# Late pointer columns of a graph-attention gather: one fp32 product per column becomes two bf16 products with row flags made four columns at a time

## What is computed

```python
hp = jnp.einsum('nf,hfo->hno', h, w)
e = leaky_relu(a_src[:, src] + a_dst[:, dst] + fc_b[0])
e = jnp.exp(e - seg_max.T[:, src])
att = e / seg_sum.T[:, src]
msg = att[:, :, None] * hp[:, dst, :]
agg = segment_sum(msg, src)        # for each head
```

## Time and profile before

| | us |
|---|---|
| median of 3 runs (12937.83 to 12961.71) | 12961.36 |
| profiled execution | 12922.84 |
| its span, first to last instruction | 12920.1 |

### The profile page before, as it was taken

The page is one execution under the profiler, slowest core; times in us unless marked ns, Lnnn a source line. Parts: engine busy times, 40 slices in busy tenths (PEclk is TensorE's granted clock), DMA queues, the critical chain, the costliest instruction groups (busy, mean ns, idle before and its releaser), DMA issues. The chain is left out here.

```text
span 12920.1 us, 83397 instructions
## 1 busy us (share of the span) xinstructions
PE 5468.6 (42%) x24919; PEld 3182.5 (25%) x25115; DVE 7098.3 (55%) x11439; ACT 3475.6 (27%) x4895; POOL 7317.1 (57%) x7495
## 2 busy tenths in 40 slices
PE   2224300029135555555537777777525665600001
PEld 1214300002124444444422222222112222200001
DVE  4663488889452222222227777777524655557761
ACT  0002333336013333333312222222100111156650
POOL 5645677758554444444455656556563455576654
PEclk5556655569556666666667777777757777755555
DMA  6101366635310000000011111111110111133431
GB/s 236 45 20 39 113 219 213 214 126 184 110 20 17 15 17 16 17 17 15 17 31 22 23 23 25 22 23 24 21 17 1 42 33 31 33 95 122 126 101 39
DMA packets 466533, 815.77 MB, mean 63 GB/s; under 512 B 229189, under 2 KB 326902, under 8 KB 415526
## 3 DMA queue, kind: packets, MB, share of 16 engines
q10 hardware_dynamic: 81600, 447.60, 8.9%
q0 software_dynamic: 236352, 156.57, 7.6%
q1 hardware_dynamic: 148134, 206.27, 4.9%
HBM read 402.58 MB, written 407.23 MB: 63 GB/s over the span
## 5 line engine op out<-in xcount | busy, mean ns | idle before, releaser
L1609 POOL DMA_INDIRECT hs<-tab_h,src_i x3136 | 2970.5, 947 | 2758.8 <-issue 1162.7
L1201 POOL DMA_INDIRECT en<-tab_s,src_i x1568 | 1569.8, 1001 | 857.3 <-issue 488.3
L1096 DVE SCALAR_TENSOR_TENSOR picked<-rank_ps,hot_hi 128x98 f32<-128x98 f32 x1568 | 313.2, 255 | 2113.8 <-remote 1123.5
L1888 PE MATMUL tp_ps<-w_pair,x 128*128 128x512 f32 x1568 | 1078.1, 776 | 534.5 <-DVE prod_b L2016 473.2
L2295 POOL DMA_INDIRECT rows_src<-out_rows,pos x784 | 750.6, 957 | 776.9 <-ACT out_rows L2338 503.1
L2317 PE MATMUL late_ps<-hot_col,hot_row 128*128 128x512 f32 x1120 | 760.6, 767 | 710.9 <-DVE hot_col L2396 626.1
L2307 POOL DMA_INDIRECT hs<-tab_h,ptr x784 | 741.3, 946 | 368.1 <-issue 252.1
L997 PE MATMUL rank_ps<-place_sb,hot_t 128*128 128x98 f32 x3136 | 843.3, 386 | 0.0
L2013 DVE TENSOR_TENSOR prod_a<-tp_ps,zz 128x768 f32<-128x768 f32 x392 | 374.6, 956 | 714.9 <-remote 563.2
L1035 PE MATMUL turn_bank<-place_sb,ident 128*128 128x98 f32 x784 | 231.7, 390 | 1196.0 <-issue 654.0
L997 PEld LDWEIGHTS rank_ps<-place_sb,hot_t 128*128 128x128 f32 x3136 | 685.5, 270 | 3.1
(11 more groups left out here) (396 smaller groups left out, 16043.0 us busy)
## 6 DMA issues: line engine op xcount, KB each, us to landing
sums<-rows ACTq DMA_DIRECT2D x98, 1088.0 KB
sums<-rows ACTq DMA_DIRECT2D x147, 512.0 KB
ev_rows<-zeros ACTq DMA_DIRECT2D x16, 3136.0 KB
en_rows<-en SPq DMA_DIRECT2D x49, 1024.0 KB
raw<-ev_rows ACTq DMA_DIRECT2D x49, 1024.0 KB
en_back<-en_rows ACTq DMA_DIRECT2D x49, 1024.0 KB
r<-in_edge_attr_2x ACTq DMA_DIRECT2D x49, 1024.0 KB
y_rows<-r ACTq DMA_DIRECT2D x49, 1024.0 KB
```

The lines of the kernel that those rows point to most:

```text
L1201: pool.indirect_dma_start(en[s][:, g, :], None, tab_s0, bass.IndirectOffsetOnAxis(ap=src_i[:, p * 2 * CH + g:p * 2 * CH + g + 1], axis=0)) ...
L1609: pool.indirect_dma_start(rows[k][:, g, :], None, tab_h, bass.IndirectOffsetOnAxis(ap=src_i[:, t * CH + g:t * CH + g + 1], axis=0)).then_i ...
L1888: nc.tensor.matmul(o, x2[k][:, a, b * EP:(b + 1) * EP], w3_cols, start=True, stop=False)
```

## The change

Each product of a late column becomes two bf16 products. The node number is split in two parts that are exact in bf16: `late_high`, a multiple of 128, and the rest, 0 to 127, which stays in `late_dst`. Four more small VectorE instructions on 560 columns make them once. Per four columns VectorE makes `row_flags` with one comparison (128x512 elements, bf16, ones and zeros). ScalarE multiplies the flags of a column by the high and by the low part (two instructions of 128 elements) into `hot_row`, which now has four buffers of two parts. `hot_col` is bf16, made as before, one instruction per column. TensorE runs four bf16 products per column (high and low, 512 and 272 columns). TensorE waits for two semaphores per column, ScalarE for the flags and for `late_added` to reach `n - 3`, VectorE ahead of new flags for ScalarE's rows of the four columns before. The number of late columns done ahead of the first turn and in each turn is rounded to a multiple of four: 148, and then 8 or 12 (mostly 8, 9 on average). ScalarE's share is placed ahead of its first turn and at the end of each turn.

```diff
-                hot_row = [sb(time, f"hot_row{n}", [EP, EP]) for n in range(2)]
-                hot_col = [sb(time, f"hot_col{n}", [EP, HCOLS]) for n in range(2)]
+                late_high = sb(time, "late_high", [EP, LATE])
+                row_flags = sb(time, "row_flags", [EP, LATE_GROUP, EP], BF16)
+                hot_row = [sb(time, f"hot_row{n}", [EP, 2, EP], BF16) for n in range(LATE_GROUP)]
+                hot_col = [sb(time, f"hot_col{n}", [EP, HCOLS], BF16) for n in range(2)]
...
-                return min(LATE, 150 + 9 * p)
+                return min(LATE, (150 + 9 * p) // LATE_GROUP * LATE_GROUP)
...
+                        pe.wait_ge(late_rows, n + 1)
                         pe.wait_ge(late_hot, n + 1)
-                        nc.tensor.matmul(late_ps[:, 0:512], hot_row[n % 2][:, :], hot_col[n % 2][:, 0:512], start=n == 0, stop=n == LATE - 1)
-                        nc.tensor.matmul(late_ps[:, 512:HCOLS], hot_row[n % 2][:, :], hot_col[n % 2][:, 512:HCOLS],
-                                         start=n == 0, stop=n == LATE - 1).then_inc(late_added, 1)
+                        for part in range(2):
+                            flags, begins, ends = hot_row[n % LATE_GROUP][:, part, :], n == 0 and part == 0, n == LATE - 1 and part == 1
+                            nc.tensor.matmul(late_ps[:, 0:512], flags, hot_col[n % 2][:, 0:512], start=begins, stop=ends)
+                            last = nc.tensor.matmul(late_ps[:, 512:HCOLS], flags, hot_col[n % 2][:, 512:HCOLS], start=begins, stop=ends)
+                        last.then_inc(late_added, 1)
...
                     H.lay(act, 2 * p + 1, 1, p)
+                    rows_of_late(late_by(p), late_by(p + 1))
+
+                def rows_of_late(first, end):
+
+                    for n in range(first, end):
+                        K.wait(act, "act", late_flagged, n // LATE_GROUP + 1, late_added, n - LATE_GROUP + 1)
+                        flags, made = row_flags[:, n % LATE_GROUP, :], hot_row[n % LATE_GROUP]
+                        nc.scalar.mul(made[:, 0, :], flags, late_high[:, n:n + 1])
+                        nc.scalar.mul(made[:, 1, :], flags, late_dst[:, n:n + 1]).then_inc(late_rows, 1)
+                rows_of_late(0, late_by(0))
...
+                        if n % LATE_GROUP == 0:
+                            K.wait(dve, "dve", late_rows, n)
+                            shape = [EP, LATE_GROUP, EP]
+                            nc.vector.tensor_tensor(row_flags[:, :, :], count_up[:, 0:EP].unsqueeze(1).to_broadcast(shape),
+                                                    pos_row[:, n:n + LATE_GROUP].unsqueeze(2).to_broadcast(shape), ALU.is_equal).then_inc(late_flagged, 1)
                         K.wait(dve, "dve", late_added, n - 1)
-                        nc.vector.tensor_scalar(hot_row[n % 2][:, :], count_up[:, 0:EP], pos_row[:, n:n + 1], late_dst[:, n:n + 1], ALU.is_equal, ALU.mult)
                         nc.vector.tensor_scalar(hot_col[n % 2][:, :], count_up, pos_late[:, n:n + 1], None, ALU.is_equal).then_inc(late_hot, 1)
```

More of the change, by code:

```diff
@@ L2201, in build @@
         with ExitStack() as st:
+            LATE_GROUP = 4
             own_e = [sb(st, f"own_e{n}", [EP, HEADS3, HCOLS]) for n in range(LISTS)]
@@ L2246, in build @@
             ptr_in, own_come, ptr_made = K.sem("ptr_in"), K.sem("own_come"), K.sem("ptr_made")
-            late_hot, late_added = K.sem("late_hot"), K.sem("late_added")
+            late_flagged, late_rows, late_hot, late_added = (K.sem(n) for n in ("late_flagged", "late_rows", "late_hot", "late_added"))
             rows_in = [K.sem(f"rows_in{s}") for s in range(2)]
```

4 lines of the change are left out of this document (added).

## The result

The changed kernel takes 12925.9 us (median of 15 runs, 12889.3 to 12943.1), the kernel before beside it 12952.8 us (15 runs, 12921.3 to 12995.9). The ratio is 0.9976, with a 95% interval of 0.9966 to 0.9985: 0.24% faster, a quarter of the forecast gain. That is inside the range, but nearer to the 44 us of rival A than to the forecast. The profiled execution has a span of 12916.5 us, against 12920.1 before.

The account below looks back on a forecast made before the run. No engine bounds the whole; VectorE and TensorE bound the second stretch, GpSimd's sends and the late count the turns. +0.4 - 44 - 60 = -104 from 12922.8 gives 12819, plus 38.5 for the median 12857, rounded 12855; range 12740 to 12945.

Parts of the forecast that it names:

- rival A: Only the second stretch gains, as the late count fills the turns up again: -44 us, 12917; chance 0.15.
- Small instructions: Four added VectorE instructions on 560 elements ahead of the first stretch: 2.5 us taken, +0.4 us in the sum.
- VectorE per column: VectorE's work on each late column: `hot_col` 0.98 us and `row_flags` 0.17, together 1.15 us.
- ScalarE: Two instructions per late column, 0.85 us, beside VectorE's 1.15; laying out chunks in the turns adds +7 us.
- late count: The count TensorE raises reaches VectorE 6.8 us or more after the product; such waits are named "remote".
- TensorE: Four bf16 products per late column take 1.0 us, hidden while a product takes up to 1.2 us.
- D: The change doesn't do what it says, TensorE at half clock or ScalarE over 1.3 us a column: 12940; chance 0.06.
- Second stretch: 9859.6 to 10038.6, GpSimd idle, no late count: 116 columns at 1.15 us instead of 1.53, -44 us.
- First stretch: 9592.8 to 9859.5, GpSimd issues `own_rows` DMAs: the late count sets 8.3 us a column, nothing gained.
- Turns: GpSimd's 49 turns of sends: cheaper columns behind the last send, -64 us in long turns, -10 in short; -60 taken.
- B: Slower, the late count spreads into short turns: 13013, up to 13200; chance 0.12.
- C: The late count belongs to the long fp32 products, so halving them shortens or ends it: 12470 or 12750; chance 0.10.

Follow-up runs that it names:

- f1: The changed kernel unedited, in a session where no count was late: 9829.5 us, ratio 0.9972 to the kernel before.
- e2: The changed kernel with six `hot_col` and six `hot_row` buffers: 12831.4 us, ratio 0.9893 to the kernel before.
- e1: The changed kernel without the low part's products, four TensorE instructions a column instead of eight, output incomplete: 12761.3 us, ratio 0.9847 to the kernel before.
- e4: The kernel before with each of its two fp32 products cut in two, 16 TensorE instructions a column instead of 8: 12989.9 us against 12957.3, one run.
- g1: The changed kernel with a one-element memset on GpSimd behind each send of the turns: 12913.5 us, ratio 0.9963 to the kernel before.
- f2: The kernel before unedited, traced in a session where no count was late: 9851.4 us, one run.
- e5: The changed kernel with ten `hot_col` and ten `hot_row` buffers: 12775.1 us, ratio 0.9905 to the kernel before.
- e7: The kernel before, in fp32, with four `hot_row` and four `hot_col` buffers instead of two: 12812.3 us, ratio 0.9937 to itself unedited.
- e8: The changed kernel with a five-element memset on GpSimd behind each `own_rows` send: 12878.8 us against 12909.1 for the kernel before, one run.
- g2: The changed kernel with ten buffers and a memset behind every send, of `own_rows` and of the turns: 12784.5 us, ratio 0.9871 to the kernel before.

## Why the prediction was wrong

*Small instructions.* 9615.49 to 9617.98, 2.5 us. As put.

*VectorE per column.* `hot_col` 1.026 us, at 0.95 to 0.98 back to back; `row_flags` 0.68. As put.

*ScalarE.* 0.39 us each, 0.30 apart, 0.6 a column where 0.85 was taken: hidden, as put. The Trainium skill's page "ScalarE: Activation LUTs" (Rules for kernel authors) puts the multiplication on VectorE, as faster per element. No run here has VectorE do this product alone, and the nearest rows are alike, 0.39 us here against 0.41 for VectorE's compare and multiply of the earlier trace rows. Where counts aren't late the move cost nothing: in f1 GpSimd's turns run nearly without a gap. Whether ScalarE's 18 instructions a turn make the late count set in sooner, no run tested.

*TensorE.* The four products of a column take 0.66 us at the full clock (e2: `late_ps` products of 0.38 and 0.28 follow each other every 0.33), where 1.0 was taken. The clock stayed at 0.95 in the second stretch and didn't fall, so *D* didn't come.

*Second stretch.* -44 forecast; from the scan to the first send -45.2 measured. 120 columns from 9875.5 to 10016.3 are 1.18 us each, two of them with a late wait; from 9881.8, where the late waits end, it is 1.14, against 1.15 forecast. Right.

*First stretch.* 28 columns in the window instead of 32, at the same 11.20. The four that are left for later are some 5 us, where +0.4 was put; the rest is right.

*Turns: the step that failed.* -60 forecast, +11 measured. The step held the number of columns behind GpSimd's last send fixed, at six in each of 22 long turns, and made each of them cheaper. Neither half of that number held. Already in the kernel before, 97 columns are behind in 21 long turns, mostly five in one, so the turn of the earlier trace rows was one of the larger ones, and the saving of 64 us was too high by about a quarter. And in the changed kernel the number didn't stay: 134 columns are behind instead of 97. Beside the two turns' sends of a pair some 11 pass, where it was mostly 13, though VectorE needs less time for each. It waits instead: "remote" before the late columns in the turns rose from 223.2 us in 43 times to 374.3 in 69. The columns behind are cheaper, as forecast, and the 37 that came to them took that back: by an estimate from these rows, 97 x (1.53 - 1.2) = 32 us saved and 37 x 1.2 = 44 us added, so +12, near the +11 measured.

What ties this to TensorE's instructions is e1 (half of them: 72 behind, turns 112 us shorter) and f1 (no late counts: no long turn). e1 halves the time of the products too, but f1 has all four of them and loses nothing by it. That is the mechanism of rival A, at 0.15: whatever VectorE saves comes back as waiting for the count. Its -44 is nearer to the -27 that came than the forecast's -104. It is in part that of *B* too, the sign of which the prediction named: the late count began inside turns that had none before, the 11 fresh ones, as if it depended on how many instructions ran rather than on time. e4 (twice the TensorE instructions) and g1 (memsets on GpSimd) point the same way, with late waits in 36 of 46 and 26 of 27 fresh turns. B's price, over 150 us, didn't come: after most short turns GpSimd still waits only 0.3 us. Why fewer columns pass isn't worked out beyond this.

The argument against A, that the late count is gone within microseconds of the last send, is true in the turns (10409.83 follows after a wait of 0.51 us) and beside the point: it says how fast the columns behind the last send go, not how many there are. In the first stretch it isn't true: in the traces of before, changed, e1, e2 and e4 late waits go on for 21 to 25 us after the last `own_rows` send.

*C* is refuted by e1, e4 and f2: fp32 or bf16, long or short products make no difference. *A's and B's rule* from the Trainium skill's page "NOTIFIC — the notification-queue block" (7.1, Overflow), an internal queue of trace records that backpressures, fits what the runs show, a fixed time for each TensorE instruction whatever its kind; no run here shows that queue, nor whether counts are late when nothing is recorded, and neither the page nor a run says why a session is free of it.

*Where the 27 us come from.* With late counts, in the two profiled executions: -45 ahead of the turns, +11 in them, and +8 in the gathers behind, which the change doesn't touch. Without: 1 us ahead of the turns, -26 in them. That both are near 27 is chance.

*Shown*: the pace of 1.40 us per TensorE instruction while `own_rows` is sent, with three instruction counts; that it isn't there in another session on the same chip, with the same GpSimd pitch; that fewer TensorE instructions (e1) and more buffers (e2, e5, e7) shorten the waits in the turns. Buffers take back only a part: this stage is 74 to 118 us shorter with them, and 497 us shorter (505 for the kernel before) where no count is late. *Open*: what outside the program makes counts late; what sets the moment at which it begins, which e4 and g1 move; why memsets between sends doubled the pace in the first stretch and not in the turns.

## What to carry to other kernels

When a wait is for a count that comes long after the work it counts, look for what sets the lateness before pricing a faster engine: vary the number of instructions per count, and see whether the pitch follows. If it does, halving the instructions' length gave nothing here where the count set the pace; halving their number or having more buffers did, and two more fp32 buffers were worth more than the whole bf16 rewrite. Then run the same kernels in another session: where no count was late, the rewrite was worth 0.28%, and neither more buffers nor memsets added to it. And a saving inside a loop that is paced by something else must be priced by what that something lets through per turn, not by how much cheaper each step has become.

## What the runs showed of the hardware that wasn't expected

While GpSimd issues indirect DMAs 1.26 us apart, the semaphore that TensorE raises arrives late by 1.40 us per TensorE instruction, weight loads included, for fp32 and bf16 alike (pitch 5.60, 11.20, 22.40 us for 4, 8, 16). TensorE itself isn't slowed: its products start 0.15 us after VectorE's row ends. In the first stretch it sets in some 20 to 30 us after the first of the sends, and it goes on for 21 to 25 us after the last; with a memset behind every send (e8, g2) about twice as many columns got through, and it ended 2 us after the last. In the turns it set in from 26 us after GpSimd's restart in the kernel before, and from 13 us in the changed one. The same kernels, on the same chip, at another time showed none of it and took 9830 to 9860 us instead of 12780 to 12960; what makes the difference is open.
